# The quantised inner tile of a gated block is transposed by a DMA in place of TensorE and ScalarE

## What is computed

```
def act_quant(x):                       # one scale for each token
    scale = 127 / clip(max(abs(x), axis=-1), 1e-5)
    return clip(round(x * scale), -128, 127) / scale
gate = silu(act_quant(n) @ ternary(w_gate).T)     # n: layer norm of x, 256 -> 1024
up   = act_quant(n) @ ternary(w_up).T             # 256 -> 1024
y    = act_quant(gate * up) @ ternary(w_down).T   # 1024 -> 256
x    = x + tanh(g_ffn) * y
```

## Time and profile before

| | |
|---|---|
| device time, median of 3 runs | 1953.72 us (1951.31, 1953.72, 1955.2) |
| profiled execution, first to last instruction (span) | 1951.5 us |
| TensorE busy | 1757.3 us (90%) |
| VectorE busy | 1658.2 us (85%) |
| ScalarE busy | 1431.7 us (73%) |
| GpSimd busy | 1052.8 us (54%) |
| mean granted TensorE clock | 0.988 |

### The profile page before, as it was taken

How to read it: one execution, slowest core, us unless ns; L and a number is a source line. 1 busy time by engine, 2 the same in 40 slices (tenths; PEclk the granted TensorE clock), 3 DMA queues, 4 the chain that set the end, 5 groups by cost and what they waited for, 6 DMA issues and landing times. The chain is left out here.

```text
span 1951.5 us, 49138 instructions
## 1 busy us (share of the span) xinstructions
PE 1757.3 (90%) x15430; PEld 1396.8 (72%) x15430; DVE 1658.2 (85%) x3609; ACT 1431.7 (73%) x2897; POOL 1052.8 (54%) x1623
## 2 busy tenths in 40 slices
PE   3899999999999999999999999999999999999984
PEld 2677777777777777777777777777777777777762
DVE  4588888888888888888888888888888888888884
ACT  3577777777777777777777777777777777777772
POOL 4455555555555545545555555555555555555541
PEclk9999999999999999999999999999999999999996
DMA  3222122122122122122122122222212212212210
GB/s 105 45 53 43 40 51 44 39 52 48 35 54 46 35 54 46 36 53 46 38 51 46 40 49 46 42 46 49 41 44 51 42 41 51 43 40 51 48 21 11
DMA packets 131684, 88.51 MB, mean 45 GB/s; under 512 B 13520, under 2 KB 131408, under 8 KB 131664
## 3 DMA queue, kind: packets, MB, share of 16 engines
q1 hardware_dynamic: 130416, 88.13, 22.3%
q10 hardware_dynamic: 1248, 0.14, 0.0%
HBM read 37.88 MB, written 16.78 MB: 28 GB/s over the span
## 5 line engine op out<-in xcount | busy, mean ns | idle before, releaser
L513 PE MATMUL psum<-k_blk,q_t 128*128 128x512 f32 x1536 | 417.8, 407 | 14.6 <-issue 12.4
L513 PEld LDWEIGHTS psum<-k_blk,q_t 128*128 128x128 f32 x1536 | 269.7, 189 | 79.2 <-issue 29.9
L1047 POOL TENSOR_SCALAR xc<-x,ln 128x256 f32<-128x256 f32 x128 | 61.2, 478 | 476.6 <-DVE ln L904 476.6
L855 DVE TENSOR_REDUCE row_max<-psum 128x8 f32<-128x1024 f32 x256 | 310.7, 1214 | 8.0 <-PE psum L513 8.0
L723 ACT ACTIVATE prob<-psum,row_max 128x128 f32<-128x128 f32 x1024 | 278.1, 386 | 16.8 <-DVE row_max L855 16.7
L1070 POOL TENSOR_SCALAR hq<-h,sm 128x1024 f16<-128x1024 f32 x128 | 143.2, 1119 | 234.5 <-DVE sm L935 234.4
L730 ACT COPY prob_t<-psum 128x1024 f32<-128x1024 f32 x256 | 262.7, 1026 | 5.0 <-PE psum L521 1.4
L521 PE MATMUL psum<-ident,prob 128*128 128x128 f32 x2048 | 255.2, 273 | 4.2 <-ACT prob L717 3.8
L521 PEld LDWEIGHTS psum<-ident,prob 128*128 128x128 f32 x2048 | 226.3, 141 | 8.7 <-ACT prob L717 5.0
L738 ACT ACTIVATE th<-psum,sm 128x512 f32<-128x512 f32 x256 | 183.2, 716 | 14.5 <-PE psum L613 12.7
L878 DVE SCALAR_TENSOR_TENSOR gu<-th,psum 128x512 f32<-128x512 f32 x256 | 174.7, 682 | 16.6 <-ACT th L738 7.4
(11 more groups left out here) (116 smaller groups left out, 3730.4 us busy)
## 6 DMA issues: line engine op xcount, KB each, us to landing
k_blk<-k_t SPq DMA_DIRECT2D x512, 64.0 KB, 2.4
c_in<-in_ctx SPq DMA_DIRECT2D x64, 256.0 KB
x_in<-in_x SPq DMA_DIRECT2D x64, 256.0 KB
out<-y SPq DMA_DIRECT2D x128, 128.0 KB
g_nat<-in_L_ffn_w_gate SPq DMA_DIRECT2D x1, 1024.0 KB, 10.2
g_nat<-in_L_ffn_w_up SPq DMA_DIRECT2D x1, 1024.0 KB, 12.4
g_nat<-in_L_ffn_w_down SPq DMA_DIRECT2D x1, 1024.0 KB, 14.4
w_nat<-in_L_xattn_Wq SPq DMA_DIRECT2D x1, 256.0 KB, 3.9
```

The source lines that it names most:

```text
L513: last = nc.tensor.matmul(dst, q_t[:, b, a, half, c.s, :], k_blk[:, w, half, c.s, 4 * b:4 * b + 4, :], start=n == 0, stop=n == len(TERMS) - 1)
L855: nc.vector.tensor_reduce(out=row_max[:, HPC * half:HPC * (half + 1)], in_=S_B[half].rearrange("p (h k) -> p h k", k=P), axis=AX.X, op=ALU ...
```

## The change

The eight transposes on TensorE (step 4) and the ScalarE copy (step 5) go. In their place SyncE issues one DMA transpose a section, from `hq` into `h_t`, which becomes two buffers. It is the first step of SyncE's body, ahead of `load_ctx` in even and of `spread_k` in odd sections, and waits for `hq_ok`. TensorE's down waits for its landing (`ht_ld`), and so does GpSimd before it writes the single `hq` again. Since nothing subtracts the 1536 any more, down ends with a ninth matmul: a tile whose first row is -1536, times a tile whose first row holds the column sums of the ternary down weights. Those sums are made once ahead of the loop by eight matmuls and a VectorE copy.

```
+ h_t = sb("h_t", [P, 2, IC, P], F16)         # was [P, INNER]
+ offset_row, wd_sum, ones16                  # [P,P], [P,D], [P,1], f16
# setup, TensorE
+ pe.wait_ge(g_ev, 3)
+ pe.wait_ge(rows0, 2)
+ for k in range(IC):
+     last = nc.tensor.matmul(bank(4)[0:1, 0:D], ones16[:, :], wd_t[:, k, :], start=k == 0, stop=k == IC - 1)
+ last.then_inc(sum_mm, 1)
# setup, VectorE
+ dve.wait_ge(sum_mm, 1)
+ nc.vector.tensor_copy(wd_sum[0:1, :], bank(4)[0:1, 0:D]).then_inc(sum_ok, 1)
# setup, GpSimd: four memsets (offset_row, wd_sum, ones16, row 0 of offset_row = -ROUND16)

# SyncE, first in body(c)
+ def hidden_t(c):
+     wait(sp, hq_ok, c.tile(3))
+     wait(sp, dn_mm, c.tile(5))
+     sp.dma_start_transpose(h_t[:, 1 - c.s, :, :], hq[:, :]).then_inc(ht_ld, 16)

# TensorE
  def gate_up(c, half):
-     wait(pe, ht_ok, c.tile(3))
- def hidden_t(c):
-     pe.wait_ge(hq_ok, c.tile(3))
-     for k in range(IC):
-         last = nc.tensor.transpose(T16[:, k * P:(k + 1) * P], hq[:, k * P:(k + 1) * P], ident16[:, :])
-     last.then_inc(h_tr, 1)
  def down(c):
-     pe.wait_ge(ht_ok, c.tile(3))
+     pe.wait_ge(ht_ld, c.even * 16 + 16 * (c.ahead + c.s - 2))
      for k in range(IC):
-         last = nc.tensor.matmul(DOWN, h_t[:, k * P:(k + 1) * P], wd_t[:, k, :], start=k == 0, stop=k == IC - 1)
+         nc.tensor.matmul(DOWN, h_t[:, 1 - c.s, k, :], wd_t[:, k, :], start=k == 0, stop=False)
+     last = nc.tensor.matmul(DOWN, offset_row[:, :], wd_sum[:, :], start=False, stop=True)
      last.then_inc(dn_mm, 1)

# ScalarE
- def hidden_t(c):
-     act.wait_ge(h_tr, c.tile(3))
-     nc.scalar.activation(h_t[:, :], T16, ACT.Copy, bias=-ROUND16).then_inc(ht_ok, 1)

# GpSimd
  def quantise_hidden(c):
-     wait(pool, h_tr, c.tile(3))
+     wait(pool, ht_ld, c.even * 16 + 16 * (c.ahead + c.s - 2))
```

More of the change, by code:

```diff
@@ L115, in flamingo_block @@
         hq = sb("hq", [P, INNER], F16)
-        h_t = sb("h_t", [P, INNER], F16)
+        h_t = sb("h_t", [P, 2, IC, P], F16)
+        offset_row = sb("offset_row", [P, P], F16)
+        wd_sum = sb("wd_sum", [P, D], F16)
+        ones16 = sb("ones16", [P, 1], F16)
         y = sb("y", [P, 2, D])
@@ L153, in flamingo_block @@
         g_ev = sem("g_ev")
+        rows0 = sem("rows0")
+        sum_mm = sem("sum_mm")
+        sum_ok = sem("sum_ok")
         with nc.Block() as block:
@@ L213, in _ @@
                 nc.gpsimd.memset(minus_half[:, :], -0.5)
+                nc.gpsimd.memset(offset_row[:, :], 0.0)
+                nc.gpsimd.memset(wd_sum[:, :], 0.0)
+                nc.gpsimd.memset(ones16[:, :], 1.0).then_inc(rows0, 1)
+                pool.wait_ge(rows0, 1)
+                nc.gpsimd.memset(offset_row[0:1, :], -ROUND16).then_inc(rows0, 1)
                 nc.gpsimd.memset(zeros[:, :], 0.0).then_inc(zeroed, 1)
@@ L330, in _ @@
                 dve.wait_ge(g_ev, 3)
+                dve.wait_ge(sum_mm, 1)
+                dve.wait_ge(rows0, 2)
+                nc.vector.tensor_copy(wd_sum[0:1, :], bank(4)[0:1, 0:D]).then_inc(sum_ok, 1)
+                dve.wait_ge(sum_ok, 1)
         kb_ld = sem("kb_ld")
@@ L381, in flamingo_block @@
             sem(n) for n in ("h_own", "h_row_max", "h_row_scale", "h_row_rcp", "h_row_factor", "y_factor"))
-        hq_ok, h_tr, ht_ok = sem("hq_ok"), sem("h_tr"), sem("ht_ok")
+        hq_ok, ht_ld = sem("hq_ok"), sem("ht_ld")
         dn_mm, y_ok = sem("dn_mm"), sem("y_ok")
@@ L391, in flamingo_block @@
         XQ16 = bank(4).bitcast(F16)
-        T16 = bank(5).bitcast(F16)
         IN_T, B6, B7 = bank(4), bank(6), bank(7)
@@ L480, in spread_k @@
                                      k_t[rows, :, :, :, :].rearrange("p a c s k -> p (a c s) k").bitcast(F32)).then_inc(kb_ld, 16)
+                def hidden_t(c):
+                    wait(sp, hq_ok, c.tile(3))
+                    hold(sp)
+                    wait(sp, dn_mm, c.tile(5))
+                    hold(sp)
+                    sp.dma_start_transpose(h_t[:, 1 - c.s, :, :], hq[:, :]).then_inc(ht_ld, 16)
                 def store(c):
@@ L488, in body @@
                 def body(c):
+                    if c.down:
+                        hidden_t(c)
                     if c.s == 0 and c.more:
@@ L651, in body @@
                             out_t(c)
-                        if c.down:
-                            hidden_t(c)
                         if c.attn:
```

## The result

The changed kernel takes 2096.71 us (median of 4 runs, 2093.88 to 2099.47) against 1954.46 us before: ratio 1.0726, 95% interval 1.0711 to 1.0741. It is slower by 142 us. The forecast had the direction and the loop, and its range (1985 to 2750 us) holds the time, but its own figure, 2289 us, put the cost at +335 us, more than twice what it is.

The account below looks back on a forecast made before the run. A loop through hq, down and the second gate and up matmuls bounds the kernel; each pair changes by 2T - 4.30 us, with T = 4.75 us +5.2, times 64 +333 us, plus 2 setup: 2289 us, range 1985 to 2750.

Parts of the forecast that it names:

- The loop: Down, second gate and up matmuls, h, hq, back to down through both sections: 29.11 us a pair, gaps 5.30 us.
- the law: A pair takes 24.07 + 2L us, L being the time from the end of hq to the start of down.
- What comes off: Removed transposes on TensorE: 0.42 us in the even section, nothing in the odd; removed ScalarE copy: nothing more.
- The ninth matmul: Added at the end of down on TensorE, on the loop: 0.13 us, twice a pair, +0.26 us.
- GpSimd's new wait: GpSimd's wait for the landing before rewriting hq: costs nothing, since down had to have that landing already.
- SyncE's queue: The transfer stands in front of spread_k, issued 2.6 us after hq: delaying it costs nothing.
- T: Transfer from issue to landing, between hq and down: taken as 4.75 us, bounds 1.72 and 10.2 us.
- The fixed part: Share of the transfer's time independent of its bytes or pieces, from the last 128 KB store: 1.35 us.
- the two hand-overs: From hq to SyncE 0.30 us and from landing to TensorE 0.07 us, together 0.37 us.
- The clock: Rival: TensorE idling before down lowers its clock, +160 us, 2449 us, or 2740 with longer transfer; chance 0.33, transfer above 6 us included.
- The rule on speed: Rival: transposing transfer between hq and down lands at copy speed, about 2.1 us; 1953 to 1995 us, chance 0.12.
- A faster version: Rival: transfer into SBUF lands in 1.72 us or less, 24 us less over the run, 1932 us; chance 0.05.

Follow-up runs that it names:

- the copy: Changed kernel with a plain copy of the same 256 KB from hq to h_t, without transposition: 1987.17 us, ratio 1.0171.
- the transfer beside the old way: Kernel before plus the transposing DMA into a tile nobody reads, GpSimd waiting for its landing too: 1958.26 us, ratio 1.0021.
- the split transfer: Changed kernel with two transposing transfers of four blocks each in place of one of eight: 2227.12 us, ratio 1.1396.
- the half tile: Changed kernel with only four of the eight blocks transposed, down using them twice: 1995.59 us, ratio 1.0214.
- the first filler: Changed kernel with TensorE's eight transposes of hq put back, unread, and a second wait and hold on GpSimd: 2096.62 us, ratio 1.0732.

## Why the prediction was right in kind and wrong in size

*The loop.* Right. The parts behind down, 13.13 and 10.68 us, did not shrink (13.31 and 10.82 in the median, with the ninth matmul in them): with the measured gaps the law gives 30.80 for 30.85 us. With three other landings (2.4 us, 3.0 us, and two issues) it is within about 0.2 us of the pair at full clock, the largest miss the copy's, 29.31 against 29.52.

*What comes off.* Right: nothing in the odd section (the wait for o_n grew by 0.42 us). TensorE would have been ready for down 2.10 and 2.58 us after hq, where the forecast had 2.10 and 2.56.

*The ninth matmul.* Right: 0.11 us a section for 0.13 (a pair 29.29 for 29.08 us), +17.5 us with its setup.

*GpSimd's new wait.* Put at nothing; it costs a little. From the last scale operation to hq it is 0.28 us in the changed kernel and 0.23 before (medians), the only difference in GpSimd's instructions there being the semaphore waited for. That is 0.05 us a section, some 6 us in all.

*SyncE's queue.* Right. spread_k is issued 2.6 us after hq as before (1036.28 to 1038.88), and the transfer beside the old way costs 4 us with GpSimd's extra wait in them.

*T, the step that failed.* "1,024 such pieces over 16 engines are 64 each, 3.4 us". The count was right, the price was not. I took 53 ns, the mean over all packets of the queue, for a packet of any size. These are packets of 512 bytes in the spreading of k, where one transfer fills 16 partitions, and of 1 KB for loads and stores. In the changed kernel's trace a packet of 512 bytes takes 62 ns, one of 1 KB 52 and one of 256 bytes 21, and the traffic 1.42 us for 3.4. The fixed part was a little low, 1.7 for 1.35 us. T is 3.1 for 4.75 us; twice the difference times 64 is 211 us. With T = 3.1 the same sum gives 64 x 1.9 = +122 us and 2 of setup, which is 2078 us, 19 less than measured. That gap is a sum of misses that partly cancel: 23 us of the clock, 8 in filling and emptying where 2 of setup were given, and steps that come to 112 in place of 122 us, above all since the two hand-overs were given as 0.37 us and took about 0.25 (gaps of 3.32 and 3.41 us less the landing). The two lower values that the text named were nearer: 2.09 us by bytes, and 2.4 us like the 64 KB copy. I chose between bounds by a mean over unlike packets. Why a packet of 512 bytes into 16 partitions takes 62 ns was not tried.

*The clock.* The forecast gave it as a rival with 160 us for waits of 3.0 and 2.6 us, and full clock otherwise; a sinking clock was one of its signs of being wrong, and came. It is neither of the two: with waits of 1.2 and 0.8 us the clock already falls now and then, 18 times at 1.3 us each, 23 us. Its price a stretch was right (1.25 us), its frequency was left out of the sum.

*The rule on speed.* What the Trainium skill says in "Advanced Engine Details and Errata", section X-Bar Transpose (TRN2), that transposing transfers are as fast as regular ones, agrees with the runs for a copy in the same pieces (3.1 against 3.0 us) and not for one in rows of 2 KB (2.4). The 350 to 400 GB/s of that section is not reached: 209 GB/s in the window above. The estimate of eight times 1309 ns, worked out from the Trainium skill's page "VectorE: DVE Perf Modes", section The three transpose paths, is far off for one transfer of eight blocks: four blocks land in 2.5 and eight in 3.1 us, so 0.15 us a block over a fixed 1.9.

*A faster version* did not come out of these runs. Even the plain copy's 2.4 us is more than the 2.15 that the loop leaves (2T - 4.30), so each transfer of the whole tile tried between hq and the down matmul of the section after it loses. Moving down a whole section later should take it off the loop; that was not tried.

## What to carry to other kernels

Before a step on a busy engine is swapped for a transfer, find the loop that it lies on and measure the gap it has to fit: here 5.3 us for two transfers, hand-overs and the two ninth matmuls included, and a transfer of 256 KB from SBUF to SBUF took 2.4 us at best. Price a transfer by its own piece size and shape from the nearest single transfer, not by the mean packet of a queue, and let both bounds speak when they disagree by a factor. And a wait on TensorE has a second price in the clock, which work that nobody reads can buy back where TensorE would only wait (24 us here).

## What was not expected of the hardware

The issue of a transposing transfer takes 1.24 to 1.27 us of SyncE's queue for four blocks as for eight, against 0.54 us for a plain copy of the same bytes. But its first packet moves 1.21 us after the issue begins, that of the plain copy 1.19, and that of the plain copy in small pieces, with an issue of 0.67 us, 1.32 us (medians): in these three the longer issue does not show in the transfer's own first packet. What stands behind it in the queue does wait for it: the split transfer's gaps are 1.3 us longer than the half tile's. One more semaphore wait on GpSimd, long met, with the count behind it (`hold`), still delays the next instruction: by 0.10 us in the first filler and 0.16 us in the transfer beside the old way.
